# Normalized tiles copied out of PSUM in a step of their own, relation counts by row tile, the embedding between outputs, and window bounds loaded one at a time

## The reference, cut to what matters

```python
for each layer:
    h = maximum(layernorm(x), 0)
    x = x + layer(h)
# attention:  e = leaky_relu(as[src] + ad[dst]); alpha = softmax of e over the edges into dst
#             out[dst] = sum alpha * (h @ W)[src];  elu;  a second one of the same kind
# relational: h = concat([x, node_emb[node_type]])
#             h = relu(mean over edges of type r of h @ w_rel[r], summed over r, + h @ w_root + b)   three times
```

## Time and profile before

| | us |
|---|---|
| three timed runs | 1849.32, 1851.18, 1852.02 |
| their median | 1851.18 |
| the profiled execution | 1853.21 |
| its span, first to last instruction | 1851.4 |
| PE busy | 1545.4 (83%) |
| DVE busy | 859.4 (46%) |
| ACT busy | 584.9 (32%) |
| POOL busy | 533.9 (29%) |
| mean granted TensorE clock | 0.915 |

### The profile page before, as it was taken

One profiled execution on the slowest core, in us unless ns is written; L12 is line 12 of the kernel. 1 busy time (PEld: TensorE's weight loads), 2 busy tenths in 40 slices (PEclk: granted clock), 3 DMA queues, 4 the chain that ended last, 5 costly groups with the idle time before them and its releaser, 6 DMA issues.

```text
span 1851.4 us, 27134 instructions
## 1 busy us (share of the span) xinstructions
PE 1545.4 (83%) x10165; PEld 1489.6 (80%) x10165; DVE 859.4 (46%) x2157; ACT 584.9 (32%) x1170; POOL 533.9 (29%) x681
## 2 busy tenths in 40 slices
PE   3985889996778898976899999999999996456786
PEld 3665789896778898976899999999999996446786
DVE  5786776324366663243634223041321223489734
ACT  2223443322244433222231222222221121356521
POOL 3233332332233322313222332323232230322221
PEclk9987999997889999987899999999999998777898
DMA  2221111122211111223111122212122221100012
GB/s 86 71 75 38 46 40 30 42 79 62 75 57 46 36 33 41 78 70 107 39 38 39 55 62 59 57 55 60 33 79 78 75 75 63 55 17 1 1 46 92
DMA packets 88053, 101.63 MB, mean 55 GB/s; under 512 B 9482, under 2 KB 80673, under 8 KB 87926
## 3 DMA queue, kind: packets, MB, share of 16 engines
q1 hardware_dynamic: 71290, 68.86, 13.0%
q10 hardware_dynamic: 16636, 31.07, 5.1%
HBM read 88.12 MB, written 11.78 MB: 54 GB/s over the span
## 4 chain that ended last, share of the span: by engine, by line
PE 60%; DVE 13%; issue 10%; DMA 8%; ACT 6%; POOL 3%; DVEq 0%; ACTq 0%; POOLq 0%; SPq 0%
PE ps L785 35%; PE ps L962 6%; PE ps L848 5%; PE ps L944 4%; DVE prob L1832 3%; DMA xl<-x_scratch 2%; PE ps L815 2%; DMA stage<-in_W 2%; DVE junk L1785 2%; PE ps L920 2%; PE ps L983 1%; DMA xl<-in_x 1%; POOL pairs L1073 1%; PE ps L1006 1%; DVE prob L1840 1%
## 5 line engine op out<-in xcount | busy, mean ns | idle before, releaser
L1073 POOL TENSOR_TENSOR pairs<-stage,pairs 128x256 fp32r<-128x256 f32 (+3 forms) x472 | 367.8, 797 | 903.4 <-ACT pairs L1162 902.4
L785 PE MATMUL ps<-pairs,XB 128*125 128x256 f32 (+2 forms) x2880 | 425.1, 309 | 50.9 <-DVE asp L1785 26.0
L785 PEld LDWEIGHTS ps<-pairs,XB 128*125 128x125 f32 (+1 forms) x2880 | 414.5, 197 | 55.1 <-issue 46.4
L785 PE MATMUL ps<-pairs,XA 128*125 128x256 f32 (+3 forms) x2655 | 378.6, 304 | 7.1 <-DVE asp L1785 6.0
L785 PEld LDWEIGHTS ps<-pairs,XA 128*125 128x125 f32 (+2 forms) x2655 | 373.7, 190 | 9.2 <-DVE asp L1785 6.4
L1162 ACT ACTIVATE pairs<-stage 128x256 fp32r<-128x256 f32 (+3 forms) x472 | 189.4, 424 | 580.6 <-PE ps L785 441.8
L1488 DVE TENSOR_TENSOR Hl<-ps,Hl 125x768 fp32r<-125x768 f32 (+3 forms) x57 | 43.6, 818 | 273.3 <-ACT Hl L1212 273.3
L848 PE MATMUL ps<-AT,Hg 125*128 125x314 f32 (+1 forms) x1080 | 163.9, 311 | 6.6 <-ACT full L1220 6.6
L848 PEld LDWEIGHTS ps<-AT,Hg 125*128 125x128 f32 (+1 forms) x1080 | 158.7, 187 | 7.7 <-ACT full L1220 7.7
L815 PE MATMUL ps<-ident,prob 125*125 125x125 f32 x475 | 87.2, 335 | 83.7 <-ACT full L1220 33.6
L815 PEld LDWEIGHTS ps<-ident,prob 125*125 125x125 f32 x475 | 76.6, 240 | 90.9 <-issue 38.6
(11 more groups left out here) (211 smaller groups left out, 1686.3 us busy)
## 6 DMA issues: line engine op xcount, KB each, us to landing
stage<-in_W SPq DMA_DIRECT2D x192, 128.0 KB, 2.3
stage<-in_rel SPq DMA_DIRECT2D x99, 192.0 KB, 2.4
stage<-in_root SPq DMA_DIRECT2D x91, 64.0 KB, 1.8
x_scratch<-xo ACTq DMA_DIRECT2D x15, 375.0 KB
xl<-x_scratch ACTq DMA_DIRECT2D x15, 375.0 KB
stage<-in_rel SPq DMA_DIRECT2D x42, 128.0 KB, 2.1
stage<-in_root SPq DMA_DIRECT2D x12, 192.0 KB, 2.4
stage<-in_W SPq DMA_DIRECT2D x12, 192.0 KB, 2.5
```

Of the source, the lines that this page charges most:

```text
L785: last = mm(o, X[:rows, xi, a, P * (s0 + t):P * (s0 + t) + m], pair(n, b), start=k == 0 and i == 0 and t * pitch % BANK == 0, stop=k == le ...
L1073: nc.gpsimd.tensor_tensor(pair(n, 1), staged(n), pair(n, 0).bitcast(F32), ALU.subtract).then_inc(*up("weights_lo", "weights lo", n))
```

## The change

- `norm_T` is split: `norm_T` is now the PE part only, and `norm_in` the copies of ACT and DVE.
- In layers 0 and 1 attention rows are transposed two ticks behind the softmax, where it was three. At the end `norm_in` 3 stands before `output` 4, then come `norm_T` 3, `early`, `norm_T` 4 with `norm_in` 4, and `late`. `FIRST_MATRIX` has an entry for layers 1, 2 and 3.
- `cr_in` comes in five DMAs of 1875 x 125 counts (one in each output step) behind the load of the next residual tile. `count_columns` goes tile by tile, tiles 0 and 1 ahead of `norm_in` 4.
- The embedding's operands are made between output 3 and `norm_in` 2, and its matmuls stand before output 4. Relation weight tiles are split at two earlier points.
- At the end of layer 2, `norm_in` 3 stands before the last tile's `combine_tile`.
- At the start the k tiles cover the first two chunks only: one before window 0, one after each of windows 0 to 10. The third chunk's matmuls stand behind the last window. `dots` go in pieces after windows 7 to 14.
- DVE loads its bounds inside each window, two register loads each. PE loads its 16 in one as before, now ahead of its first k tile.

```diff
+FIRST_MATRIX = {1: ("project", 1, 0, 256), 2: ("relation", 1, 0, 0, 384), 3: ("project", 3, 0, 384)}
+def normalized(l, d):
+    yield ("norm_T", l, d)
+    yield ("norm_in", l, d)
...
-        yield from k_tile()
         yield ("count", -1)
         yield from k_tile()
         for w in range(NW):
             yield ("count", w)
-            yield from k_tile()
+            if tiles:
+                yield from k_tile()
             if w == 6:
                 yield ("rows_lo", chunk(0, 0))
-            if w == 8:
-                yield ("dots", chunk(0, 0))
-            if w == 12:
+            if 6 < w < 12:
+                yield ("dots", chunk(0, 0), 2 * w - 14, 2 * w - 12)
+            if w == 11:
                 yield ("rows_lo", chunk(0, 1))
+            if w > 11:
+                yield ("dots", chunk(0, 1), 3 * w - 36, 3 * w - 33 + w // 14)
...
+            if not l:
+                yield ("part", first, 0, 4)
...
+    for t in range(NT + 2):
+        yield from tick(l, h, t, 2)
+        if l == 1 and t == 1:
+            yield ("split_to", FIRST_MATRIX[2], STAGED // WMAX)
...
+    yield ("output", l, 3)
+    if l == 1:
+        yield ("embed_operands",)
+    yield from normalized(l + 1, 2)
+    if l == 1:
+        yield ("split", FIRST_MATRIX[2], 0)
+        yield ("embed",)
+    yield ("norm_in", l + 1, 3)
+    yield ("output", l, 4)
+    yield ("norm_T", l + 1, 3)
+    yield ("early", FIRST_MATRIX[l + 1])
+    if l == 1:
+        yield ("count_columns", 0, 0)
+        yield ("count_columns", 0, 1)
+    yield from normalized(l + 1, 4)
+    yield ("late", FIRST_MATRIX[l + 1])
...
+                    if c and d == NT - 1:
+                        yield ("norm_in", 3, d - 1)
                     yield ("combine_tile", c, d)
                     yield ("row_part", c, d)
-                    if c and d:
+                    if c and d == NT - 1:
                         yield ("norm_T", 3, d - 1)
+                    elif c and d:
+                        yield from normalized(3, d - 1)
...
-                        act.dma_start(cr_in[:, :, :].rearrange("p t (r n) -> p t r n", r=R),
-                                      cr_scr.rearrange("(t p r) n -> p t r n", p=P, r=R)).then_inc(
-                            *up("counts_in", "counts in", by=16))
                     if d + 1 < NT:
                         load_x(i + 1)
+                    if l == 1:
+                        act.dma_start(cr_in[:, d, :].rearrange("p (r n) -> p r n", r=R),
...
-                        _, passes = nc.values_load_multi_w_load_instructions(
-                            bounds[0:1, 0, :NW + 1], engines=[mybir.EngineType.DVE], min_val=0, max_val=NW * NG // 2)
-                        _, shift_of = nc.values_load_multi_w_load_instructions(
...
-                    with dve.Fori(passes[w], passes[w + 1]) as g:
+                    upto = dve.value_load(bounds[0:1, 0, w + 1:w + 2], min_val=0, max_val=NW * NG // 2)
+                    shift = dve.value_load(bounds[0:1, 1, w:w + 1], min_val=-NW * ET, max_val=ET - SLOTS)
+                    with dve.Fori(came, upto) as g:
```

More of the change, by code:

```diff
@@ L93, in rows_of @@
     yield ("rows_lo", s)
-    yield ("dots", s)
+    yield ("dots", s, 0, DOTS)
 def wide_heads(l):
@@ L110, in wide_heads @@
     if l == 0:
-        tiles = [(h, i, k) for h, i in ((0, 0), (0, 1), (1, 0)) for k in range(6)]
+        tiles = [(i, k) for i in range(2) for k in range(6)]
         def k_tile():
[L114 to L118, removed]
-        yield from k_tile()
+            i, k = tiles.pop(0)
+            yield ("part", chunk(0, i), k, k + 1)
+            yield ("split", chunk(0, i), k + 1)
+            if k == 5:
+                yield ("rows", chunk(0, i))
         yield ("count", -1)
@@ L184, in wide_heads @@
         yield ("split", first, k1[1])
[L185 to L188, removed]
+        yield ("part", first, 4, 6)
         yield from scored(n, 4)
@@ L205, in wide_heads @@
         if h < 2:
-            yield ("dots", first)
+            yield ("dots", first, 0, DOTS)
             yield second
@@ L276, in gat_steps @@
             if t > 4 and l != 3:
[L277 to L282, removed]
+                yield from normalized(l + 1, t - 5)
+    if l == 3:
+        yield ("output", l, 3)
+        yield ("output", l, 4)
+        return
+    yield ("output", l, 3)
+    if l == 1:
[5 more added lines that the diff above has]
+    yield ("norm_in", l + 1, 3)
+    yield ("output", l, 4)
+    yield ("norm_T", l + 1, 3)
[6 more added lines that the diff above has]
+    if l == 1:
+        for d in range(2, NT):
+            yield ("count_columns", 0, d)
 def rgcn_steps():
-    yield ("embed",)
     for i in (1, 2, 3):
@@ L326, in steps @@
     for d in range(NT):
-        yield ("norm_T", 0, d)
+        yield from normalized(0, d)
     yield from gat_steps(0)
@@ L1542, in pick_columns, with count_columns @@
                 return "pick", picks_done[0] - 1
-            def count_columns(r):
-                if r == 0:
+            def count_columns(r, tiles=range(NT), junk=picked):
+                if r == 0 and tiles[0] == 0:
                     V.memset(MT[:, :, :, N:NP].bitcast(F32), 0.0).then_inc(*up("mean_step", "MT pad"))
-                    dve.wait_ge(*at("counts in"))
-                for d in range(NT):
+                for d in tiles:
                     counts = cr_in[:, d, N * r:N * r + N]
@@ L1552, in count_columns @@
                         dve.wait_ge(*at("filled", "mean_T", r - 1, d))
+                    else:
+                        dve.wait_ge(*at("counts in", d))
                     V.tensor_scalar(mean[:, d, :N], counts, EXACT, None, ALU.min)
-                    last = pick_columns(lambda j: column[:, d, j:j + 1], counts, P)
+                    last = pick_columns(lambda j: column[:, d, j:j + 1], counts, P, junk)
+                if tiles[-1] < NT - 1:
+                    return
                 dve.wait_ge(*at(*last))
@@ L1592, in _ @@
                 if kind not in ("mask_rows", "score_rows", "softmax", "attention_T", "aggregate", "elu", "elu_high", "combine", "relation_sum", "part",
-                                "split", "early", "late", "spread") or (kind == "attention_T" and s[1] < 3):
+                                "split", "early", "late", "spread", "split_to", "norm_T") or (kind == "attention_T" and s[1] < 3):
                     finish_tile()
@@ L1686, in _ @@
                         dve.wait_ge(*at("bounds"))
[L1687 to L1691 removed]
                         dve.wait_ge(*at("edge keys"))
+                        came = 0
                         continue
[L1694 to L1695 removed]
+                    upto = dve.value_load(bounds[0:1, 0, w + 1:w + 2], min_val=0, max_val=NW * NG // 2)
+                    shift = dve.value_load(bounds[0:1, 1, w:w + 1], min_val=-NW * ET, max_val=ET - SLOTS)
+                    with dve.Fori(came, upto) as g:
+                        tile = nc.s_assert_within(g * SLOTS + shift, 0, ET - SLOTS,
                                                   skip_runtime_bounds_check_because=
@@ L1780, in _ @@
                                 for v in range(2):
+                                    if not first_dot <= 2 * (s0 + t) + v < last_dot:
+                                        continue
                                     j = junks[0]
@@ L1793, in _ @@
                             G.same(("dot", junks[0] - 1), "free", q)
-                    G.same(("dot", junks[0] - 1), "vectors read", i)
-                    G.same(("dot", junks[0] - 1), "dots", s)
+                    if last_dot == DOTS:
+                        G.same(("dot", junks[0] - 1), "vectors read", i)
+                        G.same(("dot", junks[0] - 1), "dots", s)
                 elif kind == "score_sum":
```

71 lines of the change are left out of this document (38 added, 33 removed).

## The result

The changed kernel takes 1829.05 us (median of 4 runs, 1824.82 to 1830.77) where the kernel before takes 1850.32 (4 runs, 1849.32 to 1852.02). The ratio is 0.9877, with a 95% interval from 0.9859 to 0.9895. The forecast was 1830 us. The total is right by luck: two of its terms are wrong by about ten us each and cancel, as the stages show.

A forecast was written before the change was run, and what follows sets the result against it. PE was taken to stall at layer ends on one row tile's chain through DVE, POOL and ACT, and to alternate with DVE in the count. -8 - 14 - 9 + 10 = -21 from 1853.2, median 2.0 lower: 1830 us, range 1808 to 1847.

The forecast's parts named there:

- plain windows at 5.66 us: Count of edges: sign of being wrong, windows staying at 5.66 us instead of the forecast 6.4, which would mean cheap loads.
- PE waiting as long as before in front of a moved block: Layer ends: sign of being wrong, as the waits before the moved blocks were forecast to go or shrink.
- End of layer 2: Tile 3's copies ahead of tile 4's normalization cut PE's 9.63 us wait to about 2; gain 9 us, 7.5 to 10.
- End of layer 0: 48 early projection matmuls run behind tile 3's copies, before tile 4's transposes; gain 8 us, bounds 4 and 9.
- The count: Count of edges: single loads make DVE the bound; last window ends at 153.0 instead of 142.8, +10 us.
- X: Count of edges: time that two register loads add to DVE's work per window, forecast 2.6 us against 1.86 of slack.
- cheap loads: Rival, count of edges: loads cost 0.68 us each, X is 1.2, count ends 8 us earlier; 1812 us, chance 0.27.
- the -12 of the lower bound: Count of edges: at 0.3 us a register the loads hide in the slack and only removed parts count, -12.
- End of layer 1: Embedding wait hidden, 48 relation matmuls early, tile 4's rows 1.5 us later; gain 14 us, bounds 6 and 18.
- that chain: End of layer 1: embedding's operands ahead of the last output, removing PE's 6.88 us wait; about 8 us with the embedding.
- The bound of 6 us: End of layer 1: lowest gain, if two 3.6-us count transfer pieces ahead of residual tiles fall on the path.
- The slower side: Rival, count of edges: no run-ahead, loads of 1.9 us or more; 1858 us, deciding from X = 4.1; chance 0.08.

The follow-up runs named there:

- with the loads away: Changed kernel with DVE's window bounds loaded in two blocks before the first window instead of two register loads per window: 1823.78 us, ratio 0.9847 to the kernel before.
- the matmuls' move alone: Changed kernel with the embedding's matmuls moved behind tile 3's transposes on every engine: 1817.18 us in one run.
- The kernel with six loads: Changed kernel with each counting window's two register loads made three times over: 1854.90 us in one run.

## Why the prediction was right, and where it was not

The prediction had named two signs of being wrong that came: plain windows at 5.66 us (they stayed at 5.68), and PE waiting as long as before in front of a moved block (14.83 us before the embedding, where it had been 6.88).

**End of layer 2: right.** 9 forecast, 8.5 measured; undone, it cost 8.2 us of time and 8.6 of the stretch.

**End of layer 0: right in size, half right in cause.** 8 forecast, 7.0 measured. The early block is worth 4.3 of it, some two thirds. That tile 4's transposes would wait for the early block I had said ("perhaps 1 us"; they start 2.0 behind the end of `hn`, 488.40 to 490.36). The shorter lag I had not counted at all: tile 4's rows, forecast "as before", are ready 1.5 us sooner against the score matmul.

**The count: the mis-sized term.** The step that failed is "the nearest is the load of 16 registers, 1.36 us". For one register it is 0.30. With X near 0.9, the "cheap loads" rival was the true state of the loads, but its own number was wrong too: it put the end of the count 8 us earlier, and it came 1.1 earlier. It took loads within the slack for free, and they cost 6.8 us in the windows where DVE is the bound; with the loads away the last window ends 7.8 us sooner than before, the rival's number. Two smaller slips: DVE's own work in a window is 5.66 - 1.86 = 3.80 us by the rows and not 3.78, 0.3 us over the windows; and the -12 of the lower bound is added up nowhere (the parts that are named as removed come to 3.7 + 2.5 us). The rule of the Trainium skill (DMA: Bandwidth & Descriptors, section Latency and other measured facts) puts the floor of a tensor_load at about 600 ns. This trace does not agree: 30 loads have medians of 306 and 299 ns.

**End of layer 1: the step that failed.** "With that chain ahead of the last output this wait goes and is hidden by the output's 30 matmuls." On PE the embedding was put ahead of the output, so the output could not hide the operands: it waited for them. With the matmuls' move alone the stretch is 87.9 us, 17.0 under the kernel before: the 14 us were there to be had. I had worked out when the operands would be ready from a duration of 4.6 us; with POOL at work beside them they took 7.5 (847.13 to 854.67). Tile 4's rows, forecast 1.5 us later, came 9.5 later: output 4, behind the embedding, started 1.5 us later against the score matmul (58.4, where it was 56.9), its matmuls took 2.8 us longer after the pause (8.29 against 5.51), and the rest lies behind it, where tile 3's transposes and copies now stand ahead of tile 4's normalization. The bound of 6 us ("two pieces fall on the path") was broken as well: 2.6, and at most 5.6 by the other traces.

**The slower side.** The point from which loads would decide was put at X = 4.1. The kernel with six loads, at a hole of 3.49, came out 24.1 us above the changed kernel in span and level with the kernel before (1854.9 in its one run against 1852.3, measured beside it): the mechanism is real. With 2.7 us more of hole (3.49 against 0.81) the last window ends 26.4 us later, 1.8 for each of 15 windows: its X of 3.7 less the slack of 1.86. All that lies behind the count gave 21 us and not 31, so the loads decide at about X = 3.7, a hole of 3.5 us, and not at 4.1.

The sum came out because +11 and -11 cancelled. The total alone would have confirmed a story that is wrong in two of four places.

## What to carry to other kernels

A step moved to hide a wait must be looked up in the queue of every engine that takes part in it: an early place is good on the engine that makes the operands and bad on the one that uses them, if ready work stands behind. A block load's duration says little about a single one; take the loads out, or make more of them, to see whether they lie within the slack. When two terms of opposite sign are uncertain, check them stage by stage, since the total can't.

## What the runs showed of the hardware

- A one-register load on DVE's queue takes 0.30 us, a block of 16 1.36 us: some 0.07 us for each further register, an estimate from these two rows. With its two checks, a pair of loads leaves a hole of 0.81 us in the one-hots, and two more pairs bring it to 3.49.
- DVE's small steps can run up to four times longer beside work of POOL: the two `emh` steps 0.93 and 0.98 us beside weight splits (0.20 and 0.28 without), `nth` 2.07 beside the addition to a residual tile (0.53 without), and a cast of 3x625 2.08 beside that addition alone (0.47 without). Not all do: two products of L1571, 0.81 us each, keep their time beside a split of POOL at 884.69 us of the changed kernel.
- The same code can take a different time in a stretch with many matmuls while its waits repeat: in seven traces the end of layer 1 takes 99.3 to 102.2 us, its matmuls are busy 71.6 to 74.7 us at a mean granted clock of 0.81 to 0.77, and PE's wait for the embedding's operands is 14.79 to 14.91 us.
